# A four-layer block with eight streams: setup in the order of need, later weights beside the layers

## The reference, cut to what matters

```python
for l in range(4):
    x = x + tanh(g_xattn[l]) * xattn_l(layernorm(x), ctx)   # l=2 causal; l=3 only the top 51 queries of each head
    x = x + tanh(g_ffn[l]) * ffn_l(layernorm(x))
# ffn_0: router keeps 192 of 256 rows, gelu(x @ w_block)
# ffn_1: 8 experts (top 2) of width 128, silu gated, and a shared one
# ffn_2: 8 experts (top 2) of width 512, gelu, and a shared one
# ffn_3: x and weight both rounded to an FP6 grid in blocks of 32, then x @ weight.T + bias
```

## Time and profile before

| | us |
|---|---|
| median of 3 runs | 1034.54 (1033.65 to 1035.96) |
| profiled execution, its own time | 1034.86 |
| its span in the trace | 1033.0 |
| PE busy | 913.8 (88%) |
| DVE busy | 751.8 (73%) |
| ACT busy | 646.0 (63%) |
| POOL busy | 461.0 (45%) |

### The profile page before, as it was taken

The page is one execution under the profiler, slowest core; times in us unless marked ns, Lnnn a source line. Parts: engine busy times, 40 slices in busy tenths (PEclk is TensorE's granted clock), DMA queues, the critical chain, the costliest instruction groups (busy, mean ns, idle before and its releaser), DMA issues.

```text
span 1033.0 us, 22478 instructions
## 1 busy us (share of the span) xinstructions
PE 913.8 (88%) x7921; PEld 606.4 (59%) x7921; DVE 751.8 (73%) x2544; ACT 646.0 (63%) x1445; POOL 461.0 (45%) x553
## 2 busy tenths in 40 slices
PE   0379889999999999889996888999999999999873
PEld 0224345765589888357643355656469987778422
DVE  8289998776643355997798999878844356646887
ACT  0238767676686534777674666776686457786641
POOL 9822534555365203464355255555551434252332
PEclk9769999999999999999999899999999999999966
DMA  6921211101010100001112112111010010000000
GB/s 181 286 65 28 55 40 33 33 22 44 3 43 22 32 1 17 20 23 46 29 33 53 34 32 55 26 42 33 19 49 2 17 32 17 3 18 16 19 2 22
DMA packets 67037, 39.91 MB, mean 39 GB/s; under 512 B 7911, under 2 KB 64768, under 8 KB 66928
## 3 DMA queue, kind: packets, MB, share of 16 engines
q1 hardware_dynamic: 65008, 31.70, 12.0%
q0 software_dynamic: 1920, 6.78, 2.1%
HBM read 11.19 MB, written 1.05 MB: 12 GB/s over the span
## 4 chain that ended last, share of the span: by engine, by line
PE 71%; DVE 11%; POOL 7%; ACT 6%; issue 2%; DMA 1%; SPq 1%; ACTq 0%; POOLq 0%
PE A L892 12%; PE B L883 12%; PE C L738 9%; PE A L699 7%; PE A L852 6%; PE B L718 6%; DVE mx L1191 4%; PE A L685 3%; PE B L862 3%; POOL h L533 3%; ACT probs L604 3%; PE B L678 2%; PE A L823 2%; PE B L725 2%; PE A L706 2%
## 5 line engine op out<-in xcount | busy, mean ns | idle before, releaser
L1191 DVE TENSOR_REDUCE mx<-A 128x2 f32<-128x512 f32 (+1 forms) x480 | 306.9, 684 | 54.9 <-PE A L699 28.8
L604 ACT ACTIVATE probs<-B 128x512 f32<-128x512 f32 (+1 forms) x512 | 264.6, 570 | 71.2 <-PE B L718 38.2
L657 ACT ACTIVATE probs<-B,b_sb 128x256 f32<-128x256 f32 x288 | 118.9, 472 | 79.9 <-PE B L883 78.2
L529 POOL TENSOR_TENSOR rstd<-veps,mhalf 128x2 f32<-128x2 f32 x64 | 47.7, 746 | 250.2 <-DVE veps L1151 250.0
L738 PE MATMUL C<-probs,v_aug 128*9 128x256 f32 (+1 forms) x2048 | 151.2, 377 | 1.7 <-ACT probs L604 1.6
L892 PE MATMUL A<-w_sb,probs 128*128 128x128 f32 x1152 | 141.4, 277 | 0.1
L883 PE MATMUL B<-hT,w_sb 128*128 128x256 f32 x576 | 140.9, 388 | 0.1
L892 PEld LDWEIGHTS A<-w_sb,probs 128*128 128x128 f32 x1152 | 135.9, 192 | 5.7 <-issue 3.1
L699 PE MATMUL A<-k_st,q_st 64*128 64x256 bf16 (+1 forms) x1024 | 100.2, 279 | 32.8 <-DVE mx L1191 21.4
L557 POOL TENSOR_TENSOR rn<-ss,mhalf 128x32 f32<-128x32 f32 x16 | 88.0, 5501 | 90.4 <-DVE ss L1038 90.4
L883 PEld LDWEIGHTS B<-hT,w_sb 128*128 128x128 f32 x576 | 105.1, 192 | 18.7 <-issue 2.5
(11 more groups left out here) (198 smaller groups left out, 1467.1 us busy)
## 6 DMA issues: line engine op xcount, KB each, us to landing
k_st<-k_parts SPq DMA_DIRECT2D x192, 64.0 KB, 2.0
q_st<-q_parts SPq DMA_DIRECT2D x192, 64.0 KB, 2.0
w_sb<-in_w POOLq DMA_DIRECT2D x2, 2048.0 KB, 14.9
cT<-in_ctxT SPq DMA_DIRECT2D x8, 128.0 KB, 2.8
x_in<-in_x SPq DMA_DIRECT2D x8, 128.0 KB, 3.2
fc_sb<-in_fc POOLq DMA_DIRECT2D x1, 1024.0 KB, 6.3
out_x<-xs SPq DMA_DIRECT2D x8, 128.0 KB, 1.8
probs<-in_attn_w SPq DMA_DIRECT2D x1, 512.0 KB, 4.4
```

Of the source, the lines that this page charges most:

```text
L604: nc.scalar.activation(probs[s][:, part % UNIT_RING, 2 * a:2 * a + 2, 0:n], b_bank(w, a + 1)[:, 0:2 * n].rearrange("p (j q) -> p j q", j=2 ...
L657: ins = nc.scalar.activation(hid[s][:, part % UNIT_RING, c, :], b_bank(w, half + 1)[:, j * ROWS:(j + 1) * ROWS], ACT.Gelu, bias=b1_sb[:, p ...
L1191: nc.vector.tensor_reduce(mx[s][:, r, a, hp0:hp0 + n], a_bank(w, a + 1).rearrange("p (n k) -> p n k", n=n), AX.X, ALU.max).then_inc(sems[" ...
```

## The change

The setup is cut up and put in the order in which its parts are needed.

- **Loads on SP**: first the Q and K weights of layer 0 alone (128 KB), context 0, the bias columns, x 0 and the identity (`first_loads`, their own semaphore), then the V and O weights of layer 0 and the V bias of layer 0 (`value_loads`), then the other contexts and x.
- **Loads on ACT**: the gates at once; once `first_loads` have landed three of `attention_loads` (the biases, the Q and K weights of layers 1 to 3, the layer 0 router), the other three after ACT's part of the first `keys`; and `late_loads` after the `keys` of batch 3.
- **Loads on POOL**: the six `ffn_loads` two at a time at `weigh` parts 0 to 2 of batch 0 in layer 0, the `big_loads` two at a time at `weigh` parts 0 to 6 of batch 0 in layer 1. `w1` and `w2` become eight transfers of 512 KB.
- **Clearing**: DVE clears slots 0 and 1, POOL 2 and 3. `k_st` is filled with ones by one memset over all partitions; SP waits for it before the first `keys` transfers of a slot. `max_clear` copies its zeros from `q_st` rather than from `k_st`.
- **DVE's setup**: only the reorder of layer 0's Q and K weights stands ahead of the list (`first_ready`). The rest is a step `setup` in the list, behind the first `query`; POOL, ACT and PE wait for its end at their first `max_parts`, `attend` and `max_turn`.
- **The rounding weight** is loaded at a step `load_weight3` of batch 0 and rounded in fourteen steps `weight3` between the `output` steps of layer 2; step 14 turns and copies it.
- POOL's `xs = x + gate * bias` of the first norm of each layer moves from `norm` to `max_parts` part 0, and with layer 0's the load of the next x on SP.
- `TURNS_TAKEN` is written anew, with 2280 digits (17 more steps a stream; most of them do nothing but in batch 0).

```diff
-        out += norm(l) + [("turn", l, 0), ("query", l, 0)] + [("load_x", 0, 0)] * (l == 0)
+        out += norm(l) + [("turn", l, 0), ("query", l, 0)] + [("setup", 0, 0)] * (l == 0)
-        out += tiles + [("max_parts", l, 0), ("max_parts", l, 1), ("max_turn", l, 0)]
+        out += tiles + [("max_parts", l, 0)] + [("load_x", 0, 0)] * (l == 0) + [("max_parts", l, 1), ("max_turn", l, 0)]
+                out += [("weight3", 0, part) for part in range(2 * n, 2 * n + 2) if part <= FP6_PARTS]
...
+        first_loads = [
+            (wqk_in[:, 0, :, :], attn_w[:, 0, 0:2, :]),
+            (bcol[0:HALF, :, :], bias_cols.rearrange("(m a) l c -> a m l c", a=2)[0, :, :, :]),
+            (bcol[HALF:P, :, :], bias_cols.rearrange("(m a) l c -> a m l c", a=2)[1, :, :, :]),
+            (ident[:, :], ident_in)]
+        for e in range(0, EXPERTS, 2):
+            big_loads += [
+                (w1_sb[:, e:e + 2, :, :].rearrange("d e c i -> d e (c i)"), w1.rearrange("e d i -> d e i")[:, e:e + 2, :]),
+                (w2_sb[:, e:e + 2, :, :].rearrange("i e c d -> i (e c) d"),
+                 w2.rearrange("e (c i) d -> i (e c) d", c=HC)[:, e * HC:(e + 2) * HC, :])]
...
         def clear(engine, s, cleared):
             engine.memset(q_st[s][:, :, :].bitcast(F32), 0.0)
             engine.memset(v_aug[s][:, :, :, HD:VR], 1.0)
             engine.memset(work[s][:, 0:SENT], BIG)
-            engine.memset(k_st[s][:, :, :].bitcast(F32), 0.0).then_inc(zeroed, 1)
-            for row in range(0, P, HALF // MAX_TERMS):
-                ins = engine.memset(k_st[s][row:row + 1, :, :].bitcast(U32), TWO_ONES)
+            engine.memset(k_st[s][:, :, :].bitcast(U32), TWO_ONES).then_inc(cleared, 1)
...
+                if step == "weigh" and b == 0 and l < 2:
+                    for dst, src in (ffn_loads if l == 0 else big_loads)[part * 2:part * 2 + 2]:
+                        pool.dma_start(dst, src).then_inc(ffn_loaded if l == 0 else big_loaded, 16)
...
-            pe.wait_ge(w3_quantised, 1)
-            pe.wait_ge(attn_loaded, 16 * len(attention_loads))
-            nc.tensor.transpose(B[:, 0, 0:D], work_rows[0][0][:, 0, :], ident[:, :]).then_inc(w3_turned, 1)
-            pe.wait_ge(w3_copied, 1)
-            pe.wait_ge(setup_done, 1)
+            pe.wait_ge(first_loaded, 16 * len(first_loads))
+            pe.wait_ge(first_ready, 1)
...
+            dve.wait_ge(first_loaded, 16 * len(first_loads))
+            split_heads(0).then_inc(first_ready, 1)
+            dve.wait_ge(cleared_pool, SLOTS - DVE_SLOTS)
...
+            def set_up():
+                dve.wait_ge(attn_loaded, 16 * len(attention_loads))
+                dve.wait_ge(gates_done, 1)
+                ...
+                nc.vector.memset(junk[:, :, :], 0.0).then_inc(setup_done, 1)
...
+                if step == "weight3" and b == 0 and part < FP6_PARTS:
+                    if part == 0:
+                        dve.wait_ge(w3_loaded, 16)
+                    else:
+                        wait_end("weight3", part - 1)
+                    ins = fp6(part, 0, 1, w3_sb.unsqueeze(1), work_rows[0][0][:, 0:1, :])
```

More of the change, by code:

```diff
@@ L99, in stream_steps @@
         if l + 1 == SPARSE:
-            out += [("key_unit", SPARSE, 0), ("keys", SPARSE, 0), ("key_mean", SPARSE, 0), ("load_ctx", 0, 0)]
+            out += [("key_unit", SPARSE, 0), ("keys", SPARSE, 0), ("key_mean", SPARSE, 0), ("load_ctx", 0, 0), ("load_weight3", 0, 0)]
         elif l + 1 < LAYERS:
@@ L127 @@
[L127 to L131, removed]
@@ L160, in signals @@
         "load_x": {},
+        "setup": {},
+        "load_weight3": {},
+        "weight3": {"b_full": int((b, part) == (0, FP6_PARTS)), "b_read": int((b, part) == (0, FP6_PARTS))},
         "load_ctx": {},
@@ L174, in signals @@
         "maxima": {"a_full": 2, "a_read": 2},
-        "max_parts": {"m_parts_done": part},
+        "max_parts": {"m_parts_done": part, "xb_ready": int(part == 0)},
         "max_turn": {"b_full": 1, "b_read": 1, f"m_moved{s}": 16},
@@ L375, in flamingo @@
         sems = {name: sem(name) for name in SEMAPHORES}
[L376 to L379, removed]
+        first_loaded, values_loaded, gates_loaded, attn_loaded, late_loaded, w3_loaded, ffn_loaded, big_loaded = (
+            sem(name) for name in ("first_loaded", "values_loaded", "gates_loaded", "attn_loaded", "late_loaded", "w3_loaded",
+                                   "ffn_loaded", "big_loaded"))
@@ L381, in flamingo @@
+        cleared_dve, cleared_pool = sem("cleared_dve"), sem("cleared_pool")
+        gates_done, first_ready, setup_done, w3_quantised = (
+            sem(name) for name in ("gates_done", "first_ready", "setup_done", "w3_quantised"))
         rows_in = probs[0][:, 1, :, :].rearrange("p l n -> p (l n)")[:, 0:R_GB - R_BO]
         spare = probs[1][:, 0, :, :].rearrange("p l n -> p (l n)")
[L383 to L384 removed]
+        before_f = spare[:, 2 * D:6 * D].rearrange("p (t k) -> p t k", t=RT)
@@ L445, in load_ctx @@
                 sp.dma_start(cT[s][:, :], ctxT[b, :, :]).then_inc(sems[f"ctx_loaded{s}"], 16)
-            for s in range(SLOTS):
+            for i, (dst, src) in enumerate(first_loads):
+                sp.dma_start(dst, src).then_inc(first_loaded, 16)
+                if i == 0:
+                    load_ctx(0, 0)
+                if i == 2:
+                    load_x(0, 0)
+            for dst, src in value_loads:
+                sp.dma_start(dst, src).then_inc(values_loaded, 16)
+            for s in range(1, SLOTS):
                 load_ctx(s, s)
@@ L454, in _ @@
                 if step == "load_x" and b + SLOTS < BATCHES:
-                    sp.wait_ge(sems["xb_ready"], w.at_step("xb_ready", 1, "norm", b, 0, 0))
+                    sp.wait_ge(sems["xb_ready"], w.at_step("xb_ready", 1, "max_parts", b, 0, 0))
                     load_x(b + SLOTS, s)
@@ L461, in _ @@
                     load_ctx(b + SLOTS, s)
+                if step == "load_weight3" and b == 0:
+                    sp.wait_ge(sems["a_full"], w.at_step("a_full", 1, "key_mean", b, SPARSE, 0))
+                    sp.dma_start(w3_sb, w3).then_inc(w3_loaded, 16)
                 if step == "keys":
+                    if (b < SLOTS) and l == 0:
+                        sp.wait_ge(*cleared(s))
                     for n in range(3):
@@ L500, in _ @@
         def _(pool):
[L501 to L510, removed]
+            for s in range(DVE_SLOTS, SLOTS):
+                clear(nc.gpsimd, s, cleared_pool)
+            set_up = False
             w = Walk()
@@ L535, in _ @@
                     ins.then_inc(sems[f"h_ready{s}"], 1)
-                if step == "norm" and (l < LAYERS or l == 2 * LAYERS - 1):
-                    pool.wait_ge(sems[f"h_ready{s}"], w.at(f"h_ready{s}", 1))
+                if step == "weigh" and b == 0 and l < 2:
+                    for dst, src in (ffn_loads if l == 0 else big_loads)[part * 2:part * 2 + 2]:
+                        pool.dma_start(dst, src).then_inc(ffn_loaded if l == 0 else big_loaded, 16)
+                if (step == "max_parts" and part == 0) or (step == "norm" and l == 2 * LAYERS - 1):
+                    if not set_up:
+                        pool.wait_ge(setup_done, 1)
+                        set_up = True
+                    pool.wait_ge(sems[f"h_ready{s}"], w.at_step(f"h_ready{s}", 1, "norm", b, l, 0))
                     if l == 0 and b >= SLOTS:
@@ L563, in _ @@
             act.sem_inc(sems["b_read"], CREDIT["b_read"])
-            act.wait_ge(attn_loaded, 16 * len(attention_loads))
+            for dst, src in gate_loads:
+                act.dma_start(dst, src).then_inc(gates_loaded, 16)
+            act.wait_ge(gates_loaded, 16 * len(gate_loads))
             nc.scalar.activation(tg[:, :], gates[:, :], ACT.Tanh).then_inc(gates_done, 1)
-            act.wait_ge(w3_turned, 1)
-            nc.scalar.activation(w3T[:, :], B[:, 0, 0:D], ACT.Copy).then_inc(w3_copied, 1)
-            act.wait_ge(setup_done, 1)
+            act.wait_ge(first_loaded, 16 * len(first_loads))
+            for dst, src in attention_loads[:EARLY_LOADS]:
+                act.dma_start(dst, src).then_inc(attn_loaded, 16)
+            set_up = False
             w = Walk()
@@ L591, in _ @@
                                          bias=bcol[:, l, c:c + 1]).then_inc(sems["b_read"], 1)
+                if step == "keys" and (b, l) == (0, 0):
+                    for dst, src in attention_loads[EARLY_LOADS:]:
+                        act.dma_start(dst, src).then_inc(attn_loaded, 16)
+                if step == "keys" and (b, l) == (SLOTS - 1, 0):
+                    for dst, src in late_loads:
+                        act.dma_start(dst, src).then_inc(late_loaded, 16)
+                if step == "weight3" and b == 0 and part == FP6_PARTS:
+                    copy_ac(1, w3T[:, :], b_bank(w, 1)[:, 0:D])
                 if step == "query_means":
@@ L598, in _ @@
                     n = ROWS - (P * (part % RT) if l == CAUSAL else 0)
```

(23 more changed lines are left out.)

156 lines of the change are left out of this document (76 added, 80 removed).

## The result

The changed kernel takes 1025.69 us (median of 7 runs, 1023.50 to 1029.58), the kernel before 1033.65 beside it. The ratio is 0.9926 with a 95% interval of 0.9907 to 0.9944: 0.7% faster, some 8 us, where 21 were forecast and the range ended at 1023. Its profiled execution took 1025.37 us with a span of 1023.6.

What follows compares the result with a forecast made beforehand. The prediction took the setup before the first row maximum (50.37 us) as the stretch to shorten: 1034.86 - 24.0 + 0.7 + 2.0 = 1013.6, stated as 1013.3 us for the median, with an 8-in-10 range of 1004 to 1023.

Steps and rivals of the forecast that it cites:

- PE's start, the path of batch 0: Setup: PE starts at 7.6 us, POOL's split ends 11.6, norm 0 14.0, SP's q issues 19.9, `q_st` complete about 22.
- The lead, 24.0 us: First row maximum on DVE at 26.4 us instead of 50.37; bounds of the lead 16 to 27.5.
- The setup step: The `setup` step on DVE: 8.0 us taken, bounds 6.0 to 8.7, ending at 22.9; last to arrive before the first maximum.
- `ffn_loads`, 0.7 us (0 to 3): Six POOL issues in layer 0, full queues beside `q_st` transfers of batches 2 and 3: 0.7 us charged.
- `big_loads`, 2 us (0 to 9): Thirteen loads in layer 1, spread by seven `weigh` steps, delaying 64 KB transfer groups, half without slack: 2 us charged.
- POOL's issues and `weight3`, nothing: POOL's issue time falls mostly in idle time; DVE's idle time in layer 2 hides fourteen rounding steps, charged 0.
- The new order, 0 with 4 either way: The rewritten turns, where streams crowd PE and DVE: same kinds of steps in nearly the same places, so 0.
- Half given back (1021): Rival: loads beside layers 0 and 1 delay k and q transfer groups, giving back 10 us; chance 0.17.
- "Slower" (1041): Rival: `big_loads` delay every layer 1 transfer group in PE's queue, 31 us, more than the 24 gained; chance 0.05.

Runs made afterwards that it cites:

- e6: e1 with one change of order: `keys` and statistics of batches 2 and 3 ahead of turn and query of batch 1; 1008.80 us, 0.9747.
- e5: e1 with the layer 0 and 1 feed-forward loads spread too: seven transfers, issued from 25.5 to 47.2 us; 1008.99 us, 0.9745.
- e1: The changed kernel with POOL issuing the thirteen layer 2 loads one at a time behind norms, instead of in pairs at `weigh`; 1012.71 us, 0.9777.
- e2: e1 plus thirteen 4 KB loads issued by POOL where the changed kernel issues the big ones; 1012.55 us, 0.9785.
- e10: e1 with the edits of e5 and e6, the last weight's rounding replaced by one DVE copy; 1006.89 us, 0.9742 (1005.86 us with the rounding).
- e7: e1 with the order of turns of the kernel before, new steps put right behind their predecessors; 1021.18 us, 0.9860.
- e4: The kernel before with only the later weights moved to `weigh` steps, big loads in eight pieces; old setup and order; 1044.22 us, 1.0086.
- e8: e1 with `w1` and `w2` whole, 2048 KB each: seven loads behind seven norms, not thirteen behind thirteen; 1023.31 us, 0.9888.

## Why the prediction was wrong, point by point

- *PE's start, the path of batch 0.* Right, and a little early: 5.9 for 7.6; POOL's split ended at 9.96 for 11.6. But norm 0 ended at 15.1 for 14.0: `v_aug` came at 11.3, since PE waited for the 64 KB of `bv_all`, issued at 4.53 and landed 5.31 us later by the chain, in the bulk of the start. The last `q_st` issue at 22.9 for 19.9, since SP's issues stood behind POOL's later terms.
- *The lead, 24.0 us.* Measured 20.9, within the bounds of 16 to 27.5. The setup step took 6.0 us (15.9 to 21.9), its lower bound, and not the 8.0 taken. The last wait was not this step but batch 1's chain, through PE's order (e6). I had the order of steps before me and followed batch 0 alone. In that chain POOL's L538 took 2.1 us, beside DVE's setup copies, for the 0.66 of the earlier trace rows.
- *`ffn_loads`, 0.7 us (0 to 3).* Mis-sized: 3.7 (e5), and again `q_st<-mT`, not a `q_st` transfer of batches 2 and 3.
- *`big_loads`, 2 us (0 to 9): "the loads are spread by seven `weigh` steps".* This is the step that failed, in two ways. They are not spread: the only thing that spreads issues on an in-order queue is what the queue itself waits for. And the victim was not a group of k or q transfers with slack but the 16 KB of row maxima, with next to none, which I had not listed. Measured 13.0 (e1 against the changed kernel), above the 9 of its range.
- *POOL's issues and `weight3`, nothing.* Right (e2, e10).
- *The new order, 0 with 4 either way.* Mis-sized the other way: worth some 8.5 us (e7).
- *The rivals.* "Half given back (1021)" came nearest to the 1025.7: late transfers beside layers 0 and 1 it had right, the victim (a group of k or q transfers) and the size wrong. "Slower" (1041) had PE's queue as the place of the wait; where the new setup does not pay for it, the loads do make the kernel slower: e4, 1.0086. That the forecast of 1013.3 is met by e1 (1012.7) is no merit: there the small lead, the burst of the first loads and the better order cancel.
- *The Trainium skill's page "DMA: Bandwidth & Descriptors", section "Measured"*, wants 1 MiB and more for the bandwidth of a transfer, and so spoke against 512 KB pieces. In the time of this kernel the runs went the other way: e8 with larger ones is 10.6 us slower.

In sum, from the kernel before: start -20.9; loads +3.7 and +13.0; that leaves -4.2, and the run moved by 8.0. The other 4 us are put down to the order (its part behind the start) by subtraction; e7, with the loads of e1, measures 8.5 for the whole of it.

## What to carry to other kernels

Before a bulk load is moved beside the work, list every small transfer that an engine waits for at once, and ask what may stand ahead of it, in its own queue and in the others: here a burst of 3.5 MB from POOL, beside six transfers of 64 KB in SP's own queue, held 16 KB and PE for 10 us, and the same 3.5 MB one piece at a time cost no lead (e1). "Issued at step n" paces nothing on a queue without work in step n; tie such issues to instructions on which the queue truly waits. And check the end of a shortened setup for all streams, not only for the first.

## What the runs showed of the hardware

A small transfer did not overtake queued bulk of another issuing engine. The plainest case is the second burst of the changed kernel, since SP's queue held nothing else then: its last 64 KB transfers, issued up to 112.3 us, had landed in 2.0 to 2.1. The 16 KB were issued at 115.76. The packets by queue (q0 is POOL's, q1 is SP's; number of packets, MB, their time as a share of the 16 DMA engines), in the windows 116 to 118, 118 to 119 and 119 to 120 us:

```profile
q0 software_dynamic: 173, 0.58, 89.5%
...
q0 software_dynamic: 72, 0.25, 63.1%
q1 hardware_dynamic: 27, 0.01, 4.2%
...
q0 software_dynamic: 19, 0.05, 13.3%
q1 hardware_dynamic: 9, 0.00, 1.4%
```

PE went on at 120.72, 5.0 us behind the issue; in e1 its `attend` began 2.0 us behind the same issue (114.2 and 116.2).

In the large hole SP's own queue was full as well: the six `k_st` transfers of 64 KB, issued from 134.6 to 138.1, landed 4.7 to 12.6 us later. The windows of the changed kernel:

```profile
143.00:145.00 2.00, 0.00 (x0) 0.00 (x0) 0.00 (x0) 0.00 (x0) 0.00 (x0) 0.71 1.07 332
145.00:147.00 2.00, 0.00 (x0) 0.00 (x0) 0.00 (x0) 0.00 (x0) 0.00 (x0) 0.50 1.03 319
147.00:149.00 2.00, 0.00 (x0) 0.00 (x0) 0.00 (x0) 0.00 (x0) 0.00 (x0) 0.50 1.05 314
149.00:151.00 2.00, 0.63 (x5) 0.25 (x5) 0.00 (x0) 0.01 (x1) 0.00 (x0) 0.50 0.15 39
```

and its packets from 140 to 149 us:

```profile
q0 software_dynamic: 697, 2.56, 90.3%
q1 hardware_dynamic: 646, 0.29, 13.7%
```

Nearly as many packets of SP as of POOL moved, but SP's carried 0.45 KB on average and POOL's 3.7. The Trainium skill's page "DMA: Bandwidth & Descriptors", section "Queues, rings and completion order", says that a DMA engine takes turns between its queues, a packet at a time; the trace agrees. So SP's 64 KB transfers, of small packets, crept beside POOL's loads, and the 16 KB stood behind them. Here PE went on at 150.4, when both queues had run empty. In e4 the two can be told apart: PE went on at 161.21, while from 161.2 to 164 us POOL's queue still moved 331 GB/s and SP's none:

```profile
q0 software_dynamic: 253, 0.93, 101.0%
```

So it was not the end of POOL's loads that released PE there. How the 10 us of the large hole divide between the transfers ahead in SP's queue and POOL's packets no run separates.

The clock, too, was granted at 0.50 behind the large hole: PE idle from 140.2, 0.71 from 143 to 145, 0.50 from 145 on and still after its return. What that adds to the hole's length no run separates; the lead fell by 10.0 us for 10.2 of idle PE.
